# Loading the second sample's hats from ACT's queue instead of SyncE's

## The reference, cut to what matters

```
x = x + L0(gn(x))   # conditional convolutions, weights mixed per sample   (stages n0, c0)
x = x + L1(gn(x))   # in-projection, depthwise conv, permuted selective scan (n1, s1, ta, tb, o1)
x = x + L2(gn(x))   # 1x1 conv, offsets, deformable 3x3 conv, 1x1 conv     (n2, f2, d2)
x = x + L3(gn(x))   # squared ("kerv") 1x1, 3x3, 1x1 convolutions          (n3, k3)
```

```
val = v00*wy0*wx0 + v01*wy0*wx1 + v10*wy1*wx0 + v11*wy1*wx1
out = einsum('bckhw,ock->bohw', val, w) + b
```

## Time and profile before

| | |
|---|---|
| median of three runs | 1171.32 us (1164.85 to 1178.28) |
| the profiled execution's own time | 1163.98 us |
| its span (first to last instruction) | 1162.2 us |
| mean granted TensorE clock | 0.879 |
| busy: PE / DVE / ACT / POOL | 943.2 / 721.0 / 564.2 / 423.7 us |
| queue q1 (issued by SP) | 102.87 MB, 30.2% of 16 engines' span |
| queue q10 (issued by ACT) | 5.49 MB, 2.1% |
| queue q0 (issued by POOL) | 13.71 MB, 3.9% |

### The profile page before, as it was taken

The page is one execution under the profiler, slowest core; times in us unless marked ns, Lnnn a source line. Parts: engine busy times, 40 slices in busy tenths (PEclk is TensorE's granted clock), DMA queues, the critical chain, the costliest instruction groups (busy, mean ns, idle before and its releaser), DMA issues.

```text
span 1162.2 us, 19857 instructions
## 1 busy us (share of the span) xinstructions
PE 943.2 (81%) x7302; PEld 658.1 (57%) x7302; DVE 721.0 (62%) x1916; ACT 564.2 (49%) x1187; POOL 423.7 (36%) x384
## 2 busy tenths in 40 slices
PE   0686889898989889898989898988888898867523
PEld 0445656565666565665656566666665665646312
DVE  1455466595958685776768685858585765745221
ACT  0132453655555563747464656555554737351502
POOL 2014242616262624344343526262625343431201
PEclk9967869998989998898989898989899897966756
DMA  9001043252616161525343343526171525243150
GB/s 217 1 15 47 28 125 111 77 157 64 184 46 206 40 187 49 161 89 142 107 130 123 102 152 82 162 62 187 46 194 39 170 65 148 83 113 126 27 166 14
DMA packets 112085, 123.34 MB, mean 106 GB/s; under 512 B 64498, under 2 KB 99318, under 8 KB 107958
## 3 DMA queue, kind: packets, MB, share of 16 engines
q1 hardware_dynamic: 100800, 102.87, 30.2%
q0 software_dynamic: 6144, 13.71, 3.9%
q10 hardware_dynamic: 5046, 5.49, 2.1%
HBM read 84.32 MB, written 37.73 MB: 105 GB/s over the span
## 4 chain that ended last, share of the span: by engine, by line
PE 40%; DVE 13%; ACT 11%; DMA 11%; POOL 11%; issue 7%; ACTq 2%; SPq 2%; DVEq 0%; POOLq 0%
PE ps L602 38%; POOL b_yp L1235 6%; DMA y_turned<-b_yt 4%; DMA b_yp<-y_turned,b_to 4%; POOL x L1179 3%; ACT y L926 3%; DVE st L1314 2%; DVE b_adt L1281 2%; ACTq L1141 2%; POOL rs L1179 2%; ACT x L926 2%; DMA out<-xo 2%; DMA c_w<-hat_turned 2%; ACT L926 1%; SPq L1793 1%
## 5 line engine op out<-in xcount | busy, mean ns | idle before, releaser
L1235 POOL DMA_INDIRECT b_yp<-y_turned,b_to x64 | 87.1, 1361 | 315.0 <-DMA y_turned<-b_yt 300.4
L602 PE MATMUL ps<-y,inw 128*128 128x392 f32 x384 | 138.9, 505 | 0.5 <-ACT b_re L926 0.5
L1179 POOL TENSOR_TENSOR x<-x 128x392 f32<-128x392 f32 x96 | 96.0, 1017 | 107.2 <-ACT x L926 107.1
L1314 DVE BATCH_NORM_STATS2 st<-x 128x6 f32<-128x196 f32 x256 | 73.8, 351 | 83.3 <-POOL x L1179 83.3
L1179 POOL TENSOR_TENSOR rs<-ve,root 128x4 f32<-128x4 f32 x64 | 66.5, 1039 | 159.9 <-DVE ve L1285 159.4
L1281 DVE TENSOR_TENSOR c_w<-c_w,c_hat 126x2744 f32<-126x2744 f32 x32 | 96.4, 3011 | 21.5 <-DMA c_w<-hat_turned 21.5
L602 PE MATMUL ps<-c_w,c_zt 126*64 126x196 f32 x896 | 81.9, 342 | 29.0 <-DVE c_w L1281 23.2
L602 PE MATMUL ps<-w,a_S 128*32 128x384 f32 (+2 forms) x1280 | 88.7, 419 | 12.8 <-DVE a_S L1289 12.7
L602 PEld LDWEIGHTS ps<-y,inw 128*128 128x128 f32 x384 | 70.5, 194 | 46.0 <-issue 6.8
L602 PEld LDWEIGHTS ps<-c_w,c_zt 126*64 126x64 f32 x896 | 68.8, 142 | 45.9 <-issue 38.2
L926 ACT ACTIVATE y<-x,gs,rs 128x196 f32<-128x196 f32 x128 | 60.0, 539 | 43.0 <-DVE gs L1289 42.8
(11 more groups left out here) (194 smaller groups left out, 2084.6 us busy)
## 6 DMA issues: line engine op xcount, KB each, us to landing
c_w<-hat_turned SPq DMA_DIRECT2D x32, 1350.6 KB
z_turned<-c_z SPq DMA_DIRECT2D x32, 441.0 KB
c_zt<-z_turned SPq DMA_DIRECT2D x16, 882.0 KB
b_xp<-x_turned SPq DMA_DIRECT2D x32, 222.0 KB
x<-in_x SPq DMA_DIRECT2D x32, 196.0 KB, 2.7
y_turned<-b_yt SPq DMA_DIRECT2D x32, 196.0 KB
out<-xo SPq DMA_DIRECT2D x32, 196.0 KB, 3.9
hat_turned<-c_hat SPq DMA_DIRECT2D x32, 96.5 KB
```

What stands on the lines that cost most here:

```text
L602: return nc.tensor.matmul(o, l, r, start=start, stop=stop)
L1179: return nc.gpsimd.tensor_tensor(out=o, in0=x, in1=y, op=op)
L1235: nc.gpsimd.indirect_dma_start(out=YP[:, m, h].rearrange("p b d -> p (b d)"), out_offset=None, in_=y_dram[g % 2], in_offset=bass.IndirectO ...
L1314: last = nc.vector.bn_stats(st[s][:, 2 * c + b, :], x[:, c, b, :])
```

## The change

ACT gets a step d2 0 that loads `c_w[1]`; SP's d2 0 keeps `c_w[0]` alone. The waits in front of the load are the same ones: PE is done with the products of the group before, and the stored column hats of this sample have landed (in group 0 also that the ranks are ready, which use the same memory). ACT's step stands behind its last copies of `c_z` and before `b_ln`. In groups 4 to 8 and 10 to 12 its neighbours are c0 1 (`a_th`) before and k3 2 (`d_h`) behind; in groups 13 and 15 f2 5 before and k3 2 behind; in groups 1, 2, 3, 9 and 14 k3 2 (`d_h`) before and tb 3 (`b_ln`) behind; in group 0 c0 1 before and tb 3 behind. SP's order is otherwise as it was: hat stores, z stores, `xo` stores, `c_w[0]`, `c_zt`.

```diff
 PARTS = {
-    "sync": {... "d2": {0: 2, 1: 1}, "k3": {5: 1}},
+    "sync": {... "d2": {0: 1, 1: 1}, "k3": {5: 1}},
...
-               "d2": {3: 1, 5: 2}, ...                       # scalar
+               "d2": {0: 1, 3: 1, 5: 2}, ...
-        (316382, 317056, 317056),                             # PLAN, scalar, d2
+        (305637, 316382, 317056, 317056),
...
-        (3521080, 3521081, 3522080),                          # PLAN, sync, d2
+        (3521080, 3522080),
...
+        def load_hats(eng, b, g):
+
+            if g:
+                filled(eng, "acc", g - 1, H)
+            if first(g):
+                eng.wait_ge(ranked, 1)
+            eng.wait_ge(*hat_out[b].at(g))
+            eng.dma_start(c_w[b][:, :, :].rearrange("p v n -> p (v n)"),
+                          hat_dram[g % 2][b].unsqueeze(1).to_broadcast([TAPS, HW, HW * N])).then_inc(hat_in[b].sem(g), 16)
...
             def d2(i, part, g):                                # scalar
+                if i == 0:
+                    load_hats(act, 1, g)
                 if i == 3:
...
                 else:                                          # sync, d2
-                    b = part
-                    if g:
-                        filled(sp, "acc", g - 1, H)
-                    if first(g):
-                        sp.wait_ge(ranked, 1)
-                    sp.wait_ge(*hat_out[b].at(g))
-                    sp.dma_start(c_w[b][:, :, :].rearrange("p v n -> p (v n)"),
-                                 hat_dram[g % 2][b].unsqueeze(1).to_broadcast([TAPS, HW, HW * N]))\
-                        .then_inc(hat_in[b].sem(g), 16)
+                    load_hats(sp, 0, g)
```

## The result

The changed kernel takes 1251.82 us (median; 1248.3 to 1264.25) against 1171.38 us for the kernel before in the same comparison: a ratio of 1.071, 95% interval [1.065, 1.076]. It is 80 us slower, where +19 us was forecast and 1228 us was the upper end of the range.

A forecast was written before the change was run, and what follows sets the result against it. The prediction took a chain of dependent steps through the `xo` stores, with no engine full, to bound the kernel. Its terms, 1.5 + 27.5 + 2 - 12 = +19 us, took 1171.32 to 1190 us, range 1163 to 1228 us.

The forecast's parts named there:

- What bounds the kernel: Whole kernel: no engine is full; a chain of dependent steps through the `xo` stores sets the time.
- SP loses an issue, ACT gains one: Issue queues in 16 groups: 0 us for SP, +1.5 us in all for ACT's issues and wait.
- (a): `xo` stores, delayed by ACT's load on shared engines: 1.8 us later, bounds 0 and 6.2 us.
- The start row: Kernel start, both queues loading: x loads land after 4.5 us against 2.7 in the median, 1.8 us more.
- Rival B: Shared DMA engines: long hat rows go first, z and `xo` stores stand still about 5 us; +53 us, 1224 us; chance 0.18.
- (b): Sample 0's hats before DVE's first product: landing 17.6 us after issue, delaying y 2.5 us in eight tight groups.
- a sign of being wrong: Sample 0's hats: landing within 14 us of SP's issue although sample 1's are under way would refute the prediction.
- Loose groups: Groups 7, 9, 12 to 14: only the `xo` delay counts, 1.3 us in three and 1.8 us in two.
- Last group: End of the kernel: both DVE products wait for sample 0's hats, +2 us.
- What comes back: y store in the chain: most of its 15.5 us excess landing time goes, -12 us.
- Nine engines: Hat loads: one load is carried by nine of 16 DMA engines, the same nine from either queue.
- Rival C: Shared DMA engines: transfers only interleave and just issue times change; within 8 us of before, 1171 us; chance 0.24.

The follow-up runs named there:

- e5: Kernel before, but SP issues the `xo` stores behind its y store, well ahead of the next stretch's z stores; 1161.64 us, ratio 0.992.
- e2: Changed kernel, but SP loads both hats and ACT's step keeps its waits and issues only a tiny load into scratch; ratio 1.002.
- e3: Changed kernel, but ACT loads only half of sample 1's hats and SP the other half behind sample 0's; 1206.08 us, ratio 1.030.
- e9: Changed kernel, but ACT's load reads 126 rows of 10,976 bytes of the input, same total size, on 14 engines; 1226.76 us, ratio 1.051.
- e6: Kernel before, but SP issues sample 1's hat load between the z stores and the `xo` stores; 1266.05 us, ratio 1.085.
- e10: Changed kernel, but ACT's load reads 1,764 rows of 784 bytes of the input, same total size, on 14 engines; 1221.11 us, ratio 1.045.
- e4: Changed kernel, but SP issues the `xo` stores behind its y store, well ahead of the next stretch's z stores; 1182.19 us, ratio 1.010.
- e1: Changed kernel, but ACT's load of sample 1's hats stands right behind its writes of `xo`; ratio 1.003.
- e12: Changed kernel, but ACT's load stands behind its writes of `xo`, and SP issues the `xo` stores early, behind its y store; 1161.07 us, ratio 0.996.
- e7: Kernel before, but SP loads each sample's hats by nine DMAs of one tap each; 1248.5 us, ratio 1.066.

## Why the prediction was wrong

- **What bounds the kernel:** right in the main. The chain through the `xo` stores was where the time went. But "one of twelve alike" was too much: in the kernel before, the chain passed through their landing in 5 groups, with other waits close behind it (e5 took all 35.8 us of waiting away and gained 0.8%). A later `xo` soon became what everything waited for, in 13 groups, over the exponential as the prediction has it and over PE too (60.6 us).
- **SP loses an issue, ACT gains one:** right, about 0 (e2).
- **(a), the `xo` stores:** this is the step that failed. It took 1.8 us a group, from loads that run beside others at the start; measured were 6.6 us on average in 14 groups, beyond even the upper bound of 6.2. The start row does not tell what a store loses that is queued while nine engines have 154 KB each ahead of it. e3 and e9 show that a better price was at hand: the transfer's whole time on its engines, the 6.2 us between the two landings of the earlier trace rows. Fourteen groups at that price give 87 us; e6, in one queue, cost more (8.0 us a group). Rival B had the place right and 5 us for the size. Both of its signs came, ACT's wait over 90 us and no added wait of DVE; its mechanism is neither shown nor refuted (e10). It had 0.18.
- **(b), sample 0's hats:** the effect is real, but hidden here. It is 20.5 us once `xo` is out of the way (e4 over e5), near to the 20 us (8 x 2.5) of the sum. That agreement is in part luck: the 2.5 us held the 1.8 of (a), and e4's waits run from 0.4 to 5.8 us in seven groups. In the changed kernel DVE is later than the hats by itself and waits for them in 2 groups alone. The 17.6 us from issue to landing came in e4's last group (17.7 us, 1125.23 to 1142.91), but not in the changed kernel's, with 13.0 us (1196.01 to 1209.00): there SP's issue itself was held back by the `xo` stores before it. That is inside the 14 us which the prediction had named as a sign of being wrong, with ACT's load issued 7.5 us ahead (1188.55).
- **Loose groups:** they were charged 1.3 or 1.8 us each; group 7's wait for `xo`'s stores went from 0.27 to 6.42 us, so they lost as much as the others.
- **Last group:** +2 us forecast, 0.6 us measured.
- **What comes back:** -12 us was wrong too, about 4 us did. The y store's landings in the chain did fall from 49.9 to 34.3 us, as forecast. But POOL's first gather behind them got longer. In the kernel before, beside d2 of group 7, where y landed in 2.31 us, the gather took

```profile
627.38 3.29 POOL b_yp L1235
```

and 1.59 us in group 6, where y took 4.00. From the start of the store's piece of the chain to the end of the first gather it is 5.9 us in both (562.35 to 568.25, 624.76 to 630.67), and 5.9 us after as well (601.54 to 607.44): a sooner landing gained nothing in such groups. Of the 15 landings before, only the two longest cost more than that, together 4.0 us (5.28 us with 7.0 us to the gather's end, and 7.33 us with 8.8). Why the gather is longer behind a short landing is open. POOL's gathers are busy for 99.2 us after, 87.1 before: of the 15.6 us gained, 12.1 are given back. That gives 92.4 - 15.6 + 12.1 + 0.6 = 89.5 us; the spans differ by 88.5. This is bookkeeping over one execution of each kernel and takes every wait for `xo` as lost in full.
- **Nine engines:** right. The load from ACT did meet SP's stores on engines that they need (0.52 of 16 in the stretch above), and e9's shorter loss on 14 engines fits. The rule of the Trainium skill ("DMA: Bandwidth & Descriptors", section "Why a DMA increments its semaphore by 16 and not by 1"), the largest k that divides both outer sizes, gives 9 here and 14 for e9 and e10; the packets of q10 agree. That both queues use the same nine no row shows directly, but e4's late hats fit it.
- **Rival C:** its time was far off, since the place of the load was not harmless. Where the place was harmless, in e1 (1.003) and e12 (0.996), a second issuing engine made no difference. The Trainium skill ("DMA: Bandwidth & Descriptors", section "Issuing engines are not separate DMA queues") says that it only saves issue time, and these two runs agree. Which transfer comes first that section does not say, and that was the 80 us.

## What to carry to other kernels

A load moved to a second queue was not moved out of the way here: it went ahead of all that the first queue had still to issue, and held back even the z stores issued just before it. Price it by its whole time on its engines, for whichever store the chain waits for, and not by an average loss under mixed traffic. Look first at what is issued between the old and the new place of the DMA, and move the waited-for store instead, if its data is ready long before.

## What was not expected of the hardware

- Nine DMAs of one tap each, in which 14 engines read the same 10,976 bytes, reach 113 to 123 GB/s together; one DMA of nine engines that read one row each reaches 241 GB/s (e7 against the earlier trace rows). Whether the shared row or the cutting into nine DMAs is to blame, no run separates. Fourteen engines alone are not: e9's load kept each of them for 4.6 us, less than the 6.6 us of each of nine.
- SP itself can be held in issuing: two `xo` stores took 8.04 us in the changed kernel's group 6, 0.92 us in e5, where they have no z stores and no load before them. Busy engines alone do not explain it, since e6 has the same load ahead of these stores and took 1.45 us. The cause is open.
